# A two-layer vision tower in fp32 on one core: gelu rows weighted by GpSimd, layer 0's probabilities divided as rows, layer 1's projections merged and its loop written in another order

## The chip, the cores and the metric

The kernel runs on one core of a Trainium2 chip. The metric is the device time of one execution in microseconds (us), median of the runs. Engines are named as in the profile: PE is TensorE, DVE VectorE, ACT ScalarE, POOL GpSimd, SP the engine that issues the DMAs.

## What is computed

32 images give 38 tokens each (36 patches, two class tokens) of width 256. Two layers follow; each adds an attention part and a feed-forward part to the running activation `h`.

```python
h = tok(x) ; h = concat([cls_tok, h])                         # patches @ W.T + b, + positions
h = h + attn0(layernorm(h))        # rope(q), rope(k), causal softmax(q k^T * scale) @ v, then @ Wo.T ; 16 heads of 16
h = h + moe0(layernorm(h))         # 8 experts, no activation between w_in and w_out; softmax over the top 2
h = h + attn1(layernorm(h))        # full softmax; 8 value heads; 16x8 outputs mixed by a second softmax; Wf;
                                   # + relu MLP 256->512->256
def ffn1(x):                       # ternary weights: sign(W) where |W| > mean|W|/2, else 0
    g = gelu(x @ tern(W_fc).T)     # 1024 wide
    return (layernorm(g) * ln_w + ln_b) @ tern(W_proj).T
h = h + ffn1(layernorm(h))
```

## The kernel before

**Tiles.** Three images make a tile of R = 114 rows; there are T = 11 tiles, all resident in `h`. Every engine's program is written out by hand, with semaphores; steps of different tiles are interleaved so that PE always has something to do. A function such as `c2_qk(t)` exists in the program of each engine that takes part in step `c2` of tile `t`, and the order of the calls is the order of the instructions. A wait holds everything behind it on its engine.

**fp32 from two halves.** Most products run as three fp32r matmuls (`mm3`, L1895 to L1897): high half by high half, high by low, low by high. `turn_hi` (ACT, L518) writes the high half of a transposed tile to `xth`, `turn_lo` (DVE, L978) the low half to `xtl`. Transposes (L1909, L1978, L2263) and a few products are plain fp32; each of those stands as two matmuls in the trace.

**Stage A** (layer 0's attention, and the folding of each expert's two matrices into one). The loop over t = 2 to 7 is `a_step(t)`. On PE: `scores(t-1)`, the transpose of xn, half of `combine(t)` (L2010), q/k/v products, `turn_p` (L1978: the 16 heads' probabilities transposed in four groups through tb0 and tb1), the other half of `combine`, `a2_pv` (L1989: v times probabilities, output transposed, four column groups of the array at once; L1993: the sums of the probabilities, by a matrix of ones `hsum`), transposes of q and k, `a1_patch(t+1)`, `a2_wo(t-1)` (L1895 on tb). The softmax: DVE takes the maximum (L1041) and subtracts it (L1047), ACT takes exp three times, once per image of the tile, with a bias that makes the columns of the other images zero (L561), into `p_exp`. After `a2_pv` DVE takes the reciprocal of the sums (`a2_recip`, L1061) and multiplies (`a2_o`, L1066), ACT and DVE split the result (L575, L1070).

**Stage C** (experts `c1`, layer 1's attention `c2`, its MLP `c3`). The loop over i = 5 to 10 is `c_step(i)`, with tiles i to i-4 in it. `c1_gate` is a product 8 columns wide (a `product` on `wc`, six matmuls, then `gate(t,0)` copies it, L1234). `c2_qk` makes q and k (512 columns into tb1), `c2_v` v and two more columns sets (152 columns into tb0); ACT copies q and k to rows (L635), PE transposes them back. ACT scales the experts' outputs (L695), POOL adds them to `h` (L378).

**Stage D** (layer 1's feed-forward, straight-line code that begins inside the end of C). Per tile: `d1_x`, `d1_fc` (L2251, L2252), gelu on ACT (`d1_gelu`, L736) into the one buffer `gel`, `d2_turn` (L2263, eight transposes into the two banks of `score`), `d2_hi` (ACT, L748, eight instructions that also multiply by the layer norm's weight, one column of `lnwc` each), `d2_lo` (DVE, L1438, eight), `d2_proj` (L2273, L2274), `d2_centre` and `d2_out` (L1449, L1455). `d2_stats` (L1422) needs the gelu rows.

## Time and profile before

| | us |
|---|---|
| median of 3 runs (lowest, highest) | 544.42 (544.40, 547.71) |
| the profiled execution's own time | 544.11 |
| its span, first to last instruction | 542.3 |
| mean granted PE clock | 0.988 of full |
| busy: PE, DVE, ACT, POOL | 498.7, 380.1, 280.1, 194.8 |

The 1.8 us between span and time lie outside of the instructions. Busy times are of engines that work beside each other. A matmul's own duration overlaps with the next one's, so the pace of PE is read from the distance between starts.

### The profile page before, as it was taken

Reading aid. Unit: us, or ns where it says so; the run is one execution under the profiler, and the core shown is the slowest. Engines: PE = TensorE matmul, PEld = TensorE weight load, DVE = VectorE, ACT = ScalarE, POOL = GpSimd, SP = SyncE. Lnnn points to the kernel's source line nnn. Section 1 sums busy time; section 2 is a strip of 40 time slices with the busy share of each in tenths; the row PEclk is TensorE's granted clock in tenths of the full one; section 3 lists DMA queues with packets and bytes.
Section 4 is the critical chain, followed back from the end, with each engine's and each line's share of the span. In section 5 each row is a group of like instructions: output and inputs, shape, how many; then the busy total and the mean of one; then the engine's idle time right before and its main releaser. Section 6 shows DMA issues by size and latency. Waiting matters only on the chain. (4 is left out here: it accounts for less than half of the span.)

```text
span 542.3 us, 11847 instructions
## 1 busy us (share of the span) xinstructions
PE 498.7 (92%) x3814; PEld 418.8 (77%) x3814; DVE 380.1 (70%) x1009; ACT 280.1 (52%) x684; POOL 194.8 (36%) x257
## 2 busy tenths in 40 slices
PE   8989999999998888689999999999999998989994
PEld 8778877877786666468778888888888886877874
DVE  5554366466456767547898878778788787799884
ACT  4220321322223334547667776776776787665751
POOL 4232123132133311365464553543643601243311
PEclk9998999999999999999999999999999999999997
DMA  8934342432504100000000000000000000000000
GB/s 302 391 110 164 116 149 90 153 131 81 176 27 158 25 2 1 1 0 2 1 1 1 2 0 0 0 0 0 0 0 0 2 2 0 2 10 26 19 25 16
DMA packets 10992, 29.64 MB, mean 55 GB/s; under 512 B 2192, under 2 KB 3408, under 8 KB 10704
## 3 DMA queue, kind: packets, MB, share of 16 engines
q1 hardware_dynamic: 10960, 29.23, 16.0%
q8 instruction: 18, 0.29, 0.2%
q14 instruction: 14, 0.11, 0.1%
HBM read 27.98 MB, written 1.25 MB: 54 GB/s over the span
## 5 line engine op out<-in xcount | busy, mean ns | idle before, releaser
L378 POOL TENSOR_TENSOR h<-h,scaled 114x256 f32 (+1 forms) x88 | 68.5, 779 | 43.2 <-ACT scaled L695 36.5
L330 POOL TENSOR_TENSOR small<-small,half 114x1 f32<-114x1 f32 x44 | 28.6, 650 | 135.8 <-DVE small L966 135.8
L561 ACT ACTIVATE p_exp<-sc,cst 114x608 f32<-114x608 f32 x66 | 48.1, 794 | 26.8 <-DVE sc L1047 26.8
L2010 PE MATMUL bz<-ebuf 128*128 128x256 f32 x256 | 59.0, 383 | 0.0
L569 ACT ACTIVATE pt<-tb 114x456 f32<-114x456 f32 x66 | 34.4, 556 | 35.4 <-PE tb L1978 35.3
L2010 PEld LDWEIGHTS bz<-ebuf 128*128 128x128 f32 x256 | 47.9, 192 | 5.9
L1978 PE MATMUL tb<-cst,p_exp 114*114 114x114 f32 x352 | 44.1, 266 | 6.2 <-ACT pt L569 3.7
L2156 PE MATMUL score<-v,pt 114*114 114x137 f32 x352 | 48.5, 282 | 0.0
L695 ACT ACTIVATE scaled<-bank,gl 114x256 f32<-114x256 f32 x88 | 38.8, 471 | 18.1 <-PE bank L1897 10.3
L1978 PEld LDWEIGHTS tb<-cst,p_exp 114*114 114x114 f32 x352 | 35.2, 134 | 15.4 <-ACT pt L569 7.0
L2156 PEld LDWEIGHTS score<-v,pt 114*114 114x114 f32 x352 | 43.9, 178 | 1.8
L1960 PE MATMUL score<-k_exp,q_exp 64*114 64x152 f32 x528 | 41.7, 304 | 1.3 <-DVE k_exp L1261 1.3
L1960 PEld LDWEIGHTS score<-k_exp,q_exp 64*114 64x114 f32 x528 | 36.1, 178 | 6.4 <-issue 6.1
L1895 PE MATMUL bank<-we_h,xth 128*114 128x512 f32 x88 | 37.9, 430 | 1.4 <-ACT scaled L695 1.3
L518 ACT ACTIVATE xth<-bank 128x228 fp32r<-128x228 f32 x33 | 11.9, 362 | 45.9 <-PE bank L1909 42.1
L341 POOL TENSOR_TENSOR o<-o 114x512 f32<-114x512 f32 x11 | 14.0, 1272 | 59.7 <-DVE o L1027 59.7
L1896 PE MATMUL bank<-we_l,xth 128*114 128x512 f32 x88 | 35.0, 397 | 0.0
L1897 PE MATMUL bank<-we_h,xtl 128*114 128x512 f32 x88 | 35.0, 397 | 0.0
L662 ACT ACTIVATE o<-score 114x411 f32<-114x411 f32 (+1 forms) x66 | 31.5, 480 | 5.4 <-PE score L2156 4.5
L748 ACT ACTIVATE we_h<-score,lnwc 128x114 fp32r<-128x114 f32 x88 | 23.0, 373 | 15.1 <-PE score L2263 9.2
L2273 PE MATMUL tb<-wa,we_h 128*114 128x256 f32 x88 | 23.2, 299 | 6.2 <-DVE we_h L1438 6.2
L1041 DVE TENSOR_REDUCE smax<-score 114x16 f32<-114x608 f32 x22 | 17.3, 788 | 13.7 <-PE score L1960 13.7
(210 smaller groups left out, 1315.6 us busy)
## 6 DMA issues: line engine op xcount, KB each, us to landing
ebuf<-in_w_in SPq DMA_DIRECT2D x16, 512.0 KB, 4.3
ebuf<-in_w_out SPq DMA_DIRECT2D x16, 512.0 KB, 5.1
x_raw<-in_x_tiles SPq DMA_DIRECT2D x11, 342.0 KB, 3.1
out<-h SPq DMA_DIRECT2D x10, 114.0 KB
raw<-in_w_a SPq DMA_DIRECT2D x4, 256.0 KB, 4.2
ebuf<-in_fc SPq DMA_DIRECT2D x1, 1024.0 KB, 4.9
ebuf<-in_proj SPq DMA_DIRECT2D x1, 1024.0 KB, 7.0
raw<-in_w_a SPq DMA_DIRECT2D x2, 384.0 KB, 5.4
```

What stands on the lines that cost most here:

```text
L378: gp.tensor_tensor(h[0:R, t, :], h[0:R, t, :], scaled[0:R, e % 4, :], ALU.add).then_inc(moe_acc, 1)
L561: act.activation(p_exp[0:R, :, b * S:(b + 1) * S], sc[0:R], ACT.Exp, bias=cst[0:R, CB + b:CB + b + 1], scale=SCALE).then_inc(exps, 1)
L569: act.activation(pt[0:R, 4 * g:4 * g + 4, :], tb[g % 2][0:R, 0:4 * R].rearrange("p (h r) -> p h r", h=4), ACT.Copy).then_inc(pt_odd if g % ...
L662: act.activation(o1[0:R, h0:h0 + k, :], score[0:R, g % 2, 0:k * VE].rearrange("p (h d) -> p h d", h=k), ACT.Copy).then_inc(pv1_out, 1)
L695: act.activation(scaled[0:R, e % 4, :], bk[1 + e // 2 % 2][0:R, (e % 2) * D:(e % 2 + 1) * D], ACT.Copy, scale=gl[0:R, 7, e:e + 1]).then_in ...
L1895: pe.matmul(dst, lh, rh_, start=first, stop=False)
L1896: pe.matmul(dst, lh, rl_, start=False, stop=False)
L1897: return pe.matmul(dst, ll, rh_, start=False, stop=last)
L1960: last = pe.matmul(score[0:R, i, f * HQ * S:(f + 1) * HQ * S], q_exp[rows64, f].rearrange("p b x -> p (b x)")[:, b * R:(b + 1) * R], k_exp ...
L1978: last = pe.transpose(tb[g % 2][0:R, i * R:(i + 1) * R], p_exp[0:R, 4 * g + i, :], cst[0:R, CI:CI + R])
L2010: last = pe.matmul(bz[:, m * D:(m + 1) * D], ebuf[:, 0, c * D + m * P:c * D + (m + 1) * P], ebuf[:, 1, c * D:(c + 1) * D], start=(c == 0 a ...
L2156: last = pe.matmul(score[0:R, g % 2, i * VE:(i + 1) * VE], pt[0:R, place(h0 + i), :], v1[0:R, :], start=True, stop=True)
```

## The change

Five parts.

1. **Probabilities divided as rows (stage A).** ACT takes one exp over the dense 114x608 rows (`a2_exp`), DVE sums each head's row, inverts and multiplies (`a2_norm`, three instructions), ACT copies the rows three times into `p_exp` with a scale of 0 or 1 (`a2_wide`). The eight matmuls with `hsum` (16 in the trace), `a2_recip` and `a2_o` go; ACT and DVE split the output straight from PSUM (`a2_o`, `a2_lo`). In PE's loop a quarter of `combine` moves ahead of `a1_turn`.
2. **Merged products (stage C).** q, v and eight more columns are one product of 392 columns into tb1, k and 16 more one of 272 into tb0. The weights come in four DMAs for two, so `wc_in` counts to 112. `c2_qT` and `c2_kT` wait for both copies and for `c2_v` on DVE.
3. **Gate.** Four matmuls (16 columns, 8 columns, for each half) for six; DVE adds the two halves (a reduce for the copy).
4. **Gelu rows weighted (stage D).** POOL multiplies each half row of gelu by the weight row (`d2_weigh`, 114x512) into `gel_w`; `d2_turn` reads that. `d2_hi` and `d2_lo` become one instruction per half (128x456). `gel` has two buffers.
5. **Order.** `c_step` and all straight-line parts are written in another order on every engine; the two loops keep their bounds. `tern_sum(0)` is now ACT's first step after the stage A loop, `split_x(10)` stands ahead of `a1_rope(8)` on POOL.

```diff
@@ DVE @@
-            def a2_recip(t):
-                V.reciprocal(rinv0, score[:, 0, 2 * R:4 * R]).then_inc(rinv0_ready, 1)
-            def a2_o(t):
-                V.tensor_tensor(y2[:], two(score[:, 0, 0:2 * R]), two(rinv0), ALU.mult).then_inc(o_ready, 1)
+            def a2_norm(n, k):
+                if k == 0:
+                    dve.wait_ge(dense, n + 1)
+                    V.tensor_reduce(psum_rows[0:R, 0], sc[0:R], AX, ALU.add).then_inc(summed, 1)
+                elif k == 1:
...
+                    V.reciprocal(psum_rows[0:R, 1], psum_rows[0:R, 0]).then_inc(inverted, 1)
+                else:
...
+                    V.tensor_tensor(sc[0:R], sc[0:R], psum_rows[0:R, 1].unsqueeze(2).broadcast_to([R, H, S]),
+                                    ALU.mult).then_inc(scaled_rows, 1)
@@ ACT @@
+            def a2_exp(n):
+                act.wait_ge(shifted, 2 * n + 2)
+                act.activation(sc[0:R], sc[0:R], ACT.Exp, scale=SCALE).then_inc(dense, 1)
+            def a2_wide(n, batches=range(G)):
+                act.wait_ge(scaled_rows, n + 1)
...
+                    act.activation(p_exp[0:R, :, b * S:(b + 1) * S], sc[0:R], ACT.Copy,
+                                   scale=inside[0:R, b:b + 1]).then_inc(exps, 1)
@@ PE a_step @@
                 a1_v(t)
+                combine(t, (4, 5))
                 a1_turn(t - 1)
-                combine(t, (4, 5, 6, 7))
+                combine(t, (6, 7))
@@ PE c2 @@
             def c2_qk(t):
                 pe.wait_ge(t2["lo"], t + 1)
-                product(tb[1][0:R, :], xth[1], xtl[1], wc, C_QK, 2 * D, (0, 2 * D)).then_inc(qk1_mm, 1)
+                since(pe, pt_odd, 2 * (t + T))
+                product(tb[1][0:R, 0:WQ], xth[1], xtl[1], wc, C_QK, W4, (0, WQ)).then_inc(qk1_mm, 1)
             def c2_v(t):
-                pe.wait_ge(q_ready, 2 * (t + T) + 2)
-                product(tb[0][0:R, 2 * R:2 * R + W2], xth[1], xtl[1], wc, C_V, W2, (0, W2)).then_inc(v1_mm, 1)
+                pe.wait_ge(t2["lo"], t + 1)
+                product(tb[0][0:R, 0:D + H], xth[1], xtl[1], wc, C_QK, W4, (WQ, W4)).then_inc(v1_mm, 1)
@@ POOL @@
+            def d2_weigh(t, halves):
...
+                for q in halves:
+                    gp.wait_ge(gelu, 2 * t + q + 1)
+                    if q == 0:
+                        since(gp, gT_mm, 2 * t)
+                    cols = slice(q * 512, (q + 1) * 512)
+                    gp.tensor_tensor(gel_w[0:R, cols], gel[t % 2][0:R, cols], lnw_row[0:R, cols], ALU.mult).then_inc(weighted, 1)
@@ DVE d2_lo @@
-                    for c in range(4):
-                        k = 4 * q + c
-                        last = V.scalar_tensor_tensor(gtl[:, k, :], score[:, q, c * R:(c + 1) * R], lnwc[:, k:k + 1],
-                                                      gth[:, k, :].bitcast(F32), ALU.mult, ALU.subtract)
+                    V.tensor_tensor(gtl[:, 4 * q:4 * q + 4, :], score[:, q, 0:4 * R].rearrange("p (c r) -> p c r", c=4),
+                                    gth[:, 4 * q:4 * q + 4, :].bitcast(F32), ALU.subtract).then_inc(gT_lo, 1)
```

**PE in the loop of stage A**, from the last product for v (bank2) to the transposes of q and k; L1978 and L2031 are the transposes of the probabilities, L2010 and L2059 `combine`. In the kernel before:

```order
L1897 MATMUL bank2<-wa,xtl0 114x256
L1978 MATMUL tb0<-cst,p_exp 114x114 x4
L1978 MATMUL tb1<-cst,p_exp 114x114 x4
L2010 MATMUL bz<-ebuf 128x256 x8
L1989 MATMUL score<-pt,scaled 32x114 x16
L1993 MATMUL score<-pt,scaled 32x228 x8
L1909 MATMUL tb1<-cst,o1 128x114 x2
L1909 MATMUL bank1<-cst,o1 128x114 x2
```

The same place in the changed kernel:

```order
L1950 MATMUL bank2<-wa,xtl0 114x256
L2059 MATMUL bz<-ebuf 128x256 x4
L2031 MATMUL tb0<-cst,p_exp 114x114 x4
L2031 MATMUL tb1<-cst,p_exp 114x114 x4
L2059 MATMUL bz<-ebuf 128x256 x4
L2042 MATMUL score<-pt,scaled 32x114 x16
L1962 MATMUL tb1<-cst,o1 128x114 x2
L1962 MATMUL bank1<-cst,o1 128x114 x2
```

A quarter of `combine` (x4, eight matmuls in the trace) moved ahead of the transposes of the probabilities, a quarter is left behind them, and the matmuls with the ones (32x228) are gone.

**DVE in the same loop**, from the maximum of the scores to the low half of the attention's output (xtl1). In the kernel before:

```order
L1041 TENSOR_REDUCE smax<-score 114x16
L1047 TENSOR_TENSOR sc<-score,smax 114x304 x2
L978 TENSOR_TENSOR xtl0<-bank0,xth0 128x228
L1021 TENSOR_TENSOR o1<-bank1,cst 114x512
L1056 COPY pt<-tb1 114x456
L1078 TENSOR_TENSOR we_l<-bz,we_h 128x2x256
L1061 RECIPROCAL att<-score 128x228
L1066 TENSOR_TENSOR y2<-score,att 128x228
L1035 TENSOR_TENSOR k_exp<-bank1,cst 128x456
L1070 TENSOR_TENSOR xtl1<-y2,xth1 128x228
```

The same place in the changed kernel:

```order
L1092 TENSOR_REDUCE smax<-score 114x16
L1098 TENSOR_TENSOR sc<-score,smax 114x304 x2
L1029 TENSOR_TENSOR xtl0<-bank0,xth0 128x228
L1113 TENSOR_REDUCE psum_rows<-sc 114x16
L1116 RECIPROCAL psum_rows<-psum_rows 114x16
L1119 TENSOR_TENSOR sc<-sc,psum_rows 114x608
L1072 TENSOR_TENSOR o1<-bank1,cst 114x512
L1107 COPY pt<-tb1 114x456
L1132 TENSOR_TENSOR we_l<-bz,we_h 128x2x256
L1086 TENSOR_TENSOR k_exp<-bank1,cst 128x456
L1124 TENSOR_TENSOR xtl1<-score,xth1 128x228
```

The reciprocal and the product that stood between the expert's low half and the first half of k_exp are gone; three instructions on the 608 columns of `sc` stand ahead of rope (L1072), and the low half is now taken from `score`.

**ACT at the start of stage D**, from the softmax of tile 9 (p_exp) on; the load at L792 or L736 is for gelu, that at L595, L667 or L720 for exp. In the kernel before:

```order
L736 ACT_TABLE_LOAD
L736 ACTIVATE ebuf<-bank1 114x512
L736 ACTIVATE ebuf<-bank2 114x512
L667 ACT_TABLE_LOAD
L667 ACTIVATE mx<-mx 114x128
L736 ACT_TABLE_LOAD
L736 ACTIVATE ebuf<-bank1 114x512
L736 ACTIVATE ebuf<-bank2 114x512
L667 ACT_TABLE_LOAD
L667 ACTIVATE mx<-mx 114x128
L736 ACT_TABLE_LOAD
```

The same place in the changed kernel:

```order
L792 ACT_TABLE_LOAD
L792 ACTIVATE ebuf<-bank1 114x512
L595 ACT_TABLE_LOAD
L595 ACTIVATE p_exp<-sc,cst 114x16x38 x3
L792 ACT_TABLE_LOAD
L792 ACTIVATE ebuf<-bank2 114x512
L792 ACTIVATE ebuf<-bank1 114x512
L792 ACTIVATE ebuf<-bank2 114x512
L720 ACT_TABLE_LOAD
L792 ACT_TABLE_LOAD
L720 ACT_TABLE_LOAD
L792 ACT_TABLE_LOAD
```

Before there are five loads of a table behind the stage C loop, after there are seven.

## Rows read from the trace of the kernel before

**Rows 1.** Busy us in stretches: span, then PE, PEld, DVE, ACT, POOL; clock, DMA.

```profile
71.20:169.80 98.60, 93.29 (x821) 78.65 (x820) 54.20 (x106) 26.72 (x55) 26.74 (x30) 1.00 0.37 120
169.80:231.30 61.50, 48.68 (x515) 37.99 (x514) 41.70 (x100) 25.84 (x52) 18.70 (x23) 1.00 0.05 13
231.30:292.20 60.90, 56.35 (x375) 45.86 (x375) 46.90 (x124) 38.77 (x92) 34.67 (x37) 0.97 0.00 1
292.20:418.30 126.10, 126.10 (x891) 107.22 (x890) 101.32 (x295) 91.58 (x234) 58.88 (x84) 1.00 0.00 0
...
476.20:538.50 62.30, 54.06 (x356) 45.78 (x354) 52.77 (x180) 35.95 (x119) 19.96 (x32) 0.98 0.07 20
```

**Rows 2.** Who PE waited for, whole run: us in total, times, longest.

```profile
PE tb L2273 <- DVE we_h L1438: 6.2, 5, 2.9
...
PE bank L1909 <- DVE xn L971: 3.5, 8, 0.7
...
PE tb L1895 <- DVE xtl L1070: 2.0, 6, 0.3
```

**Rows 3.** Timeline of PE, one turn of the stage A loop: start, us, line.

```profile
101.19 3.63 PE L2010 MATMUL bz<-ebuf 128*128 128x256 f32 x16
...
105.56 0.95 PE L1993 MATMUL score<-pt,scaled 114*32 114x228 f32 x16
106.44 0.41 PE L1909 MATMUL tb<-cst,o 114*128 114x114 f32 x2
...
110.66 1.82 PE L1960 MATMUL score<-k_exp,q_exp 64*114 64x152 f32 x24
...
118.81 0.94 PE L1978 MATMUL tb<-cst,p_exp 114*114 114x114 f32 x8
...
120.92 3.63 PE L2010 MATMUL bz<-ebuf 128*128 128x256 f32 x16
```

**Rows 4.** Groups of instructions: xcount | busy us, mean ns | idle before.

```profile
L561 ACT ACTIVATE p_exp<-sc,cst 114x608 f32<-114x608 f32 x66 | 48.1, 794 | 26.8 <-DVE sc L1047 26.8
...
L569 ACT ACTIVATE pt<-tb 114x456 f32<-114x456 f32 x66 | 34.4, 556 | 35.4 <-PE tb L1978 35.3
...
L1438 DVE SCALAR_TENSOR_TENSOR we_h<-score,lnwc,we_h 128x114 fp32r<-128x114 f32 x88 | 22.7, 324 | 3.8 <-ACT we_h L748 3.8
...
L1061 DVE RECIPROCAL att<-score 128x228 f32<-128x228 f32 x11 | 17.4, 1583 | 4.0 <-PE score L1993 4.0
L1041 DVE TENSOR_REDUCE smax<-score 114x16 f32<-114x608 f32 x22 | 17.3, 788 | 13.7 <-PE score L1960 13.7
...
L341 POOL TENSOR_TENSOR o<-o 114x512 f32<-114x512 f32 x11 | 14.0, 1272 | 59.7 <-DVE o L1027 59.7
L1056 DVE COPY pt<-tb 114x456 f32<-114x456 f32 x22 | 13.9, 632 | 12.5 <-PE tb L1978 11.6
```

**Rows 5.** Timeline of PE in the stage C loop.

```profile
347.52 0.17 PE L1895 MATMUL bank<-wc,xth 128*114 128x8 f32 x1
...
348.04 0.31 PE L1895 MATMUL tb<-wc,xth 128*114 128x152 f32 x1
...
348.68 0.57 PE L1909 MATMUL bz<-cst,raw 114*128 114x114 f32 x4
...
359.52 0.39 PE L1896 MATMUL tb<-wc,xth 128*114 128x512 f32 x1
...
360.67 0.63 PE L2156 MATMUL score<-v,pt 114*114 114x137 f32 x4
```

**Rows 6.** Timeline of ACT in stage D.

```profile
474.55 1.28 ACT L736 ACT_TABLE_LOAD   x1 [2.42 <-issue]
...
528.02 1.26 ACT L736 ACTIVATE ebuf<-bank 114x512 f32<-114x512 f32 x2
531.98 2.08 ACT L748 ACTIVATE we_h<-score,lnwc 128x114 fp32r<-128x114 f32 x8 [2.70 <-PE score L2263]
```

**Rows 7.** Timeline of PE, the last tile's last product.

```profile
535.22 0.37 PE L2273 MATMUL tb<-wa,we_h 128*114 128x256 f32 x1 [2.88 <-DVE we_h L1438]
```

More of the change, by code:

```diff
@@ L584, in _ @@
             a1_x(0)
+            act.activation(inside[0:R], cst[0:R, CB:CB + G], ACT.Exp).then_inc(init, 1)
             a1_v(0)
@@ L733, in d1_gelu @@
                     if q == 0:
-                        since(act, gT_mm, 2 * t)
-                        since(act, g_stat, 4 * t - 2)
-                    act.activation(gel[0:R, q * 512:(q + 1) * 512], bk[1 + q][0:R, :], ACT.Gelu).then_inc(gelu, 1)
+                        since(act, weighted, 2 * t - 2)
+                        since(act, g_stat, 4 * t - 6)
+                    act.activation(gel[t % 2][0:R, q * 512:(q + 1) * 512], bk[1 + q][0:R, :], ACT.Gelu).then_inc(gelu, 1)
             def d2_hi(t, halves=(0, 1)):
@@ L1505, in _ @@
[L1505 removed]
+            gate(0, 0)
             plus_eps(n1, 1)
[L1507 to L1510 removed]
+            a1_k(10, (0,))
+            gate(0, 1)
+            a1_k(10, (1,))
+            a2_lo(9)
             c1_normed(1)
             c1_stats(2)
[L1513 to L1516 removed]
             gate(0, 2)
[L1518 removed]
+            gate(0, 3)
@@ L1707, in _ @@
             mix(8, 12)
-            d1_x(1)
+            normed1(10)
             d2_stats(0, (0,))
+            c2_x(10)
             d1_norm(2)
             d0_stats(3)
+            d1_x(1)
+            d2_stats(0, (1,))
+            c3_res(7)
+            c2_v(10, (0,))
+            aggr(nD, 3)
+            d2_aggr(0)
+            mix(9, 0)
+            mix(9, 1)
+            d2_eps(0)
+            plus_eps(nD, 3)
+            c2_v(10, (1,))
+            mix(9, 2)
+            c3_sum(8)
+            mix(9, 3)
@@ L1786, in _ @@
-            mix(10, 11)
-            aggr(nD, 6)
-            d2_out(0)
-            d1_x(4)
+            keep_bias()
+            d2_lo(0, (1,))
+            d2_stats(2, (1,))
+            aggr(nD, 6)
+            d2_aggr(2)
+            mix(10, 9)
+            d2_eps(2)
+            plus_eps(nD, 6)
+            keep_sums()
+            d2_centre(0)
+            d2_lo(1, (0, 1))
+            d1_x(4)
+            mix(10, 10)
+            d2_out(0)
+            mix(10, 11)
+            d1_norm(6)
@@ L1802, in _ @@
-            d2_out(1)
+            c3_stats(10)
+            d1_x(6)
+            aggr(n4, 10)
+            plus_eps(nD, 7)
+            d2_out(1)
+            plus_eps(n4, 10)
+            d1_norm(7)
+            d2_aggr(3)
+            c3_normed(10)
+            d2_eps(3)
+            d2_lo(3, (0, 1))
             d2_centre(2)
-            d2_lo(3, (0,))
-            aggr(nD, 7)
-            d2_lo(3, (1,))
+            d0_stats(8)
+            d2_stats(4, (0, 1))
+            aggr(nD, 8)
             d2_out(2)
-            d2_aggr(3)
@@ L2096, in c1_gate @@
                 pe.wait_ge(t1["lo"], t + 1)
-                product(bk[0][0:R, 256:256 + E], xth[0], xtl[0], wc, C_G, E, (0, E)).then_inc(gate_mm, 1)
+                for c in range(DC):
+                    pe.matmul(bk[0][0:R, 256:256 + 2 * E].rearrange("p (a e) -> p a e", a=2), xth[0][:, c, :],
+                              wc[:, :, C_G + c * E:C_G + (c + 1) * E], start=(c == 0), stop=False)
+                    last = pe.matmul(bk[0][0:R, 256:256 + E], xtl[0][:, c, :], wc[:, 0, C_G + c * E:C_G + (c + 1) * E],
+                                     start=False, stop=(c == DC - 1))
+                last.then_inc(gate_mm, 1)
             def c1_moe(t, pairs):
```

1158 lines of the change are left out of this document (579 added, 579 removed).

## The prediction

> **What bounds the kernel now.** I read the busy times by stretch first [rows 1], then what PE waited for [rows 2], then timelines where the change works, and last the groups for prices. The reader is to compare PE's busy time with each stretch's length. From 292.2 to 418.3 (the stage C loop, six turns of 21.0 us) PE is busy for all of 126.1 us: it sets the pace, and only taking work off PE, or a new wait, changes it. In the five turns of the stage A loop from 71.2 to 169.8 PE idles 98.6 - 93.3 = 5.3 us, 1.06 a turn. From 169.8 to 231.3, where stage A drains, it idles 12.8 us, from 231.3 to 292.2 4.6 us, and in the last stretch 8.2 us. So PE bounds the loops; between them and at the end chains over DVE and ACT do. In the waits, stage D shows as PE waiting 6.2 us for the low halves of gelu, 2.9 of them once, and stage A as PE waiting for xn (0.44 on average) and for the low half of the attention's output (0.33) [rows 2].
>
> **The sum** is made against the profiled execution's 544.1 us; the median is 0.3 above that.
>
> **Stage A's loop.** One turn takes 120.92 - 101.19 = 19.73 us [rows 3]. Removed on PE: the matmuls with the ones, from 105.56 to 106.44, 0.88 us. Removed on DVE: the reciprocal of 1.58 us [rows 4] and a product of about 0.4; both stand between `a2_pv` and `a2_wo`, and ahead of `a1_k` and the moments of the next tile. With nearly 2 us gone from that path, the wait of `a2_wo` (0.33) and that for xn (0.44) end [rows 2]. Saved: 0.88 + 0.33 + 0.44 = 1.65 us a turn, 9.9 in six turns; tile 0, outside of the loop, gives 0.9.
>
> The price is on the other side of the tile: the softmax. From the end of the scores (110.66 + 1.82 = 112.48) to the transposes of the probabilities (118.81) PE has 6.3 us of other work [rows 3]; the quarter of `combine` put ahead of them adds 3.63 / 2 = 1.8, so the cover is 8.1 us. Behind it must fit: maximum 0.79 and subtraction, about as long, exp 0.79 once, sum 0.79 (as the maximum of the same 608 columns), inversion 0.2, product 0.8, three copies of 0.79 [rows 4]: 6.6 us, and with six handoffs of 0.1 (my estimate) 7.2. It fits with 0.9 to spare, so I cost it at nothing here. The unseen ones are bounded by rows: the copy between 0.56 (456 columns) and 0.79 (the exp, 608 columns), the product between 0.63 (456 columns) and 1.6 (the reciprocal's price), each taken by the row nearest in columns. At the upper end the chain is 8.0 and still fits; what isn't covered comes back six times.
>
> **Where stage A drains** (tiles 7 to 10) that cover is thin, and the chain is the time: per tile it gains 0.79 + 0.79 + 0.2 + 0.8 = 2.6 us and handoffs, and loses 0.88 + 1.58 + 0.4 = 2.9. I take the two as equal. `tern_sum(0)`, now ACT's first step, and POOL's `split_x(10)` ahead of `a1_rope(8)` each hold a chain by some 2 us there, which the other of the two partly covers. Against that, two of the experts' products of tile 0 now stand in a wait for the softmax, and the gate of tile 0 too. I take 1.3 us saved; the ends are 4 lost and 5 saved, of the 12.8 us idle.
>
> **Stage C, all eleven tiles.** Six matmuls of 8 columns take 0.52 us, six of 152 columns 0.64, so neither costs in proportion to its columns: a step lasts 0.09 to 0.11 at least. One of 512 columns takes (360.67 - 359.52) / 5 = 0.23 [rows 5]. Now: gate 4 steps for 6, 0.17 less. Merged products: 6 x 0.23 + 0.64 = 2.02 before; after, 392 and 272 columns in proportion to 512, 6 x (0.176 + 0.122) = 1.79, 0.23 less. Together 0.40 a tile, 4.4 in eleven. Since PE never idles in this loop, all of it shows if no wait comes. The transposes of q and k now wait for two copies by ACT and both sums by DVE, but an expert's product of 1.4 us (6 x 0.23) was put between. In the straight-line turns (4.6 us idle [rows 1]) the same cover stands where PE waited; I take 1.2 saved, between 1 lost and 3 saved.
>
> **Stage D.** `d2_hi` is eight instructions in 2.08 us [rows 6], `d2_lo` eight in 8 x 0.26 = 2.06 (22.7 / 88 [rows 4]). After: two each; ACT's at 0.56 (the same 456 columns), DVE's at 0.63, its copy of 456 columns; the dearest row for it is four of 0.324, 1.3. DVE, 52.8 of 62.3 us busy, gets 0.8 us a tile free, ACT 1.0. From the start of `d2_hi` to the product that needs the last `d2_lo` it now takes 535.22 - 531.98 = 3.24 us [rows 6, 7]; after, 0.56 + 0.56 + 0.63 + handoffs = 1.95. That is 1.3 less for each tile. PE's waits there are 3.3 us in four and 2.9 in the last [rows 2]: the four go, the last falls by 1.3. That gives 4.6, and 0.9 of the idle left comes with it: 5.5 us.
>
> Added is POOL's work: 2 x 1.27 us a tile (114x512, the same shape as `a1_rope`'s [rows 4]), 28 us in all, on an engine with 20.0 of 62.3 us used in the last stretch. It lies between gelu and the transposes. For the last tile gelu ends at 529.3 [rows 6], so the second product would end near 531.9, with its transposes at 532, where they end now: hidden. With a second gelu buffer, gelu of the next tile doesn't wait.
>
> The Trainium skill speaks against this part: its GPSIMD Engine Reference, section 4.1, sends elementwise products to VectorE, since GpSimd is about twice as slow with two inputs. The trace has 1.27 us on POOL for 512 columns, and DVE's product would not be half the problem, as DVE is the fuller engine; by that rule the first rival would decide.
>
> Two more loads of an activation table stand in the new order. One lasts 1.28 us [rows 6]; ACT idles enough there, so nothing to 2.6 us, taken as nothing. The Trainium skill (ScalarE: Activation LUTs, What ACT_TABLE_LOAD costs) adds a drain of 1.38 us to each load; 2.42 us of idle stand ahead of the one in the rows, which agrees in kind. By it ACT would lose 5.3 us, not 2.6.
>
> **Sum:** 0.9 + 9.9 + 1.3 + 4.4 + 1.2 + 5.5 = 23.2; 544.1 - 23.2 = 520.9, with the 0.3 of the median 521.2; I say 521.
>
> **Rivals.**
> 1. POOL sets the pace of stage D. For: 2.54 us a tile on top of two powers and an addition, in an engine that works in order; if DVE's use of memory slows it to 2 us a product, it needs over 5.5 us a tile, as now. Against: it idles two thirds of the stretch. Then stage D gives nothing, 521 + 5.5 = 526.5.
> 2. The softmax isn't covered. For: six handoffs, and DVE does other steps between. Against: 0.9 us to spare. With 1 us of wait in ten tiles 531.
> 3. In stage C the transposes wait for the copies, 0.6 us a tile, 528. For: three engines in a row within 1.4 us. Against: ACT was built in right ahead.
> 4. More goes than I count: the drain of stage A gives its 5, stage D its 8.2. 515. For: both idle sums exist. Against: chains are left in both.
> 5. Slower: in the stage C loop the new order makes a ring, where DVE's `c2_v(1)` stands behind `mix(0)`, that behind ACT's copy of the last attention output, and PE's transposes behind all. From 23.2 / 11 = 2.1 us of wait a tile on it eats the gain. At 3 us it costs 33, 554. For: none of these waits existed, and PE had no idle in 126 us, so each adds in full. Against: by the rows each link is under 0.6 us.
>
> **Chances.** Forecast 0.61, rival 1 0.14, rival 2 0.07, rival 3 0.07, rival 4 0.05, rival 5 0.06, a third of it beyond 550. A measurement of this kernel can tell about 1%, 5.4 us, from no change: faster than 539, slower than 550. Faster 0.94, within 1% 0.04, slower 0.02. The range of 8 in 10 takes in rivals 1 to 4 and the unknown prices: 512 to 532.
>
> **What would show it.** Right: no 32x228 matmuls; turns of 18.1 us in stage A's loop and of 20.6 in stage C's, with PE still busy throughout; DVE's low halves of gelu as 22 instructions of 0.6 us; under 3 us idle in PE's last stretch before the final tile. Wrong: PE waiting for p_exp inside stage A's loop (rival 2), for the rows or for v ahead of the transposes (3, 5), or for POOL's products in stage D (1).

## The result, and the profile after

The changed kernel takes 553.19 us (median of 13 runs, 548.02 to 555.67), the kernel before 544.27 in as many; the ratio is 1.0142, with a 95% interval of 1.0113 to 1.0170. It is slower by 1.4%, where 521 us had been forecast. The profiled execution has a span of 553.1 us at a mean granted PE clock of 0.958; before it was 542.3 us at 0.988. Executions of one program differ with the granted clock (five of these 13 took 548.0 to 549.9 us at 0.967 to 0.975, the other eight, the profiled one among them, 552.1 to 555.7 at 0.958 to 0.963), and the ratios leave out those over 1.5% above the fastest of their kernel (two of e1's ten, one of e8's).

The stretches of the changed kernel first (columns as in [rows 1]): the same five turns of the stage A loop, the way from the scores of tile 7 to the small product for the ternary sums (tb<-th,ones), the stage C loop, then up to the scores of tile 10, and the rest.

```profile
72.60:164.50 91.90, 88.14 (x742) 75.90 (x740) 54.01 (x111) 29.56 (x60) 26.73 (x30) 1.00 0.38 124
164.53:237.57 73.04, 54.56 (x446) 44.26 (x445) 38.59 (x95) 27.99 (x55) 16.93 (x21) 0.81 0.06 18
298.60:426.20 127.60, 126.43 (x878) 108.50 (x877) 102.09 (x296) 95.02 (x240) 71.44 (x84) 1.00 0.00 0
426.20:460.80 34.60, 31.09 (x207) 27.02 (x205) 25.03 (x78) 26.70 (x61) 15.51 (x19) 0.95 0.00 1
460.80:553.10 92.30, 79.38 (x529) 67.65 (x528) 72.16 (x169) 44.77 (x95) 52.04 (x59) 0.97 0.05 15
```

- The loop of stage A does what was forecast, nearly: 91.9 us for five turns where [rows 1] has 98.6.
- From the scores of tile 7 to the ternary sums it takes 73.0 us; before, the same way was 169.85 to 231.14, 61.3 us, at a clock of 1.00. Now PE idles 73.0 - 54.6 = 18.5 us there and gets a clock of 0.81. That is the largest change of the whole trace, and in the wrong direction.
- The stage C loop takes 127.6 us for six turns, 126.0 before; PE is busy for 126.4 of them, and yet the turns are slower.
- From the scores of tile 10 to the end it takes 92.3 us for 95.6 (446.7 to 542.3 before).

Summed by these marks, after minus before, in us: the start (to the scores of tile 1) +2.8, the loop of stage A -8.1, between the loops +11.7, unrolled stage C -0.2, its loop +1.6, from there to the scores of tile 10 +6.2, the rest -3.3; in all +10.7, for 10.8 between the spans.

The last two of these sums don't hold the same work. The new order has eight matmuls of 512 columns of `d1_fc` ahead of the scores of tile 10 that stood behind them before (L2251 and L2252 80 times behind the mark, L2310 and L2311 72 times); at 0.23 us each that is 1.9 us moved from one stretch to the other. Without them it is +4.3 up to the scores of tile 10 and -1.4 for the rest. Taken together, the two take 126.9 us for 124.0.

Who PE waited for (as [rows 2]):

```profile
PE bank L1948 <- DVE xtl L1029: 6.2, 3, 3.2
PE tb L2031 <- ACT p_exp L614: 6.1, 3, 2.8
...
PE tb L2031 <- issue: 4.0, 3, 3.3
...
PE score L2322 <- DVE we_h L1496: 2.0, 3, 1.1
```

Three more lines of before belong beside these:

```profile
PE score L1955 <- DVE y L1066: 2.6, 2, 1.8
PE tb L1978 <- ACT p_exp L561: 2.4, 2, 1.6
...
PE score L2263 <- DVE we_h L1438: 1.8, 2, 1.1
```

Three waits for `p_exp` (L614) take 6.1 us, where two took 2.4 (L561), and one for the softmax of tile 9 (put down as "issue") takes 3.3. The two waits for the attention's output behind the reciprocal and the product (y, L1066), 2.6 us, are gone. The wait for the low halves of gelu was 6.2 us at the product [rows 2] and 1.8 at the transposes (L2263), and is 1.7 (L2332) and 2.0 (L2322) now; but PE waits 2.7 us for gelu itself (ebuf, L792), which no line of before has.

### The profile page after: what moved, and what is told of

It is laid out like the page before. It is cut to its first block, busy times and chain, and to the rows that moved or that the text cites. A ratio compares the mean times of both kernels' runs of the same rounds, so it can differ in the third digit from the quotient of the medians.

```text
span 553.1 us, 11435 instructions
## 1 busy us (share of the span) xinstructions
PE 499.7 (90%) x3616; PEld 425.2 (77%) x3616; DVE 378.0 (68%) x954; ACT 282.2 (51%) x643; POOL 234.9 (42%) x277
## 4 chain that ended last, share of the span: by engine, by line
PE 42%; ACT 5%; DVE 4%; issue 4%; POOL 0%; DVEq 0%; ACTq 0%; POOLq 0%
PE score L2215 7%; PE bz L2245 3%; PE tb L2031 3%; PE score L2013 3%; PE bank L1948 2%; PE bank L1950 2%; PE bank L1949 2%; PE tb L2332 2%; PE bank L2310 2%; PE tb L2333 2%; PE bz L1962 2%; PE bank L2311 2%; PE bz L2227 2%; PE score L2322 1%; PE bz L1948 1%
## 5 line engine op out<-in xcount | busy, mean ns | idle before, releaser
L2059 PE MATMUL bz<-ebuf 128*128 128x256 f32 x256 | 60.1, 384 | 0.0
L2031 PE MATMUL tb<-cst,p_exp 114*114 114x114 f32 x352 | 47.4, 281 | 13.4 <-ACT p_exp L614 6.1
L2031 PEld LDWEIGHTS tb<-cst,p_exp 114*114 114x114 f32 x352 | 37.9, 142 | 22.7 <-ACT p_exp L614 6.7
L2059 PEld LDWEIGHTS bz<-ebuf 128*128 128x128 f32 x256 | 47.6, 193 | 5.7
L2013 PE MATMUL score<-k_exp,q_exp 64*114 64x152 f32 x528 | 43.0, 310 | 0.1
L2013 PEld LDWEIGHTS score<-k_exp,q_exp 64*114 64x114 f32 x528 | 37.6, 185 | 5.5 <-issue 4.5
L614 ACT ACTIVATE p_exp<-sc,inside 114x608 f32<-114x608 f32 x33 | 24.1, 794 | 21.5 <-DVE sc L1119 21.5
L715 ACT ACTIVATE o<-score 114x411 f32<-114x411 f32 (+1 forms) x66 | 31.3, 479 | 7.3 <-PE score L2215 5.8
L430 POOL TENSOR_TENSOR ebuf<-ebuf 114x512 f32<-114x512 f32 x22 | 28.3, 1296 | 12.2 <-PE score L2322 9.3
L345 POOL TENSOR_TENSOR small<-small,half 114x2 f32<-114x2 f32 x11 | 21.9, 1991 | 21.6 <-DVE small L1249 21.6
L1107 DVE COPY pt<-tb 114x456 f32<-114x456 f32 x22 | 13.9, 632 | 25.0 <-PE tb L2031 25.0
```

The costliest lines, as they stand in the source:

```text
L715: act.activation(o1[0:R, h0:h0 + k, :], score[0:R, g % 2, 0:k * VE].rearrange("p (h d) -> p h d", h=k), ACT.Copy).then_inc(pv1_out, 1)
L2013: last = pe.matmul(score[0:R, i, f * HQ * S:(f + 1) * HQ * S], q_exp[rows64, f].rearrange("p b x -> p (b x)")[:, b * R:(b + 1) * R], k_exp ...
L2031: last = pe.transpose(tb[g % 2][0:R, i * R:(i + 1) * R], p_exp[0:R, 4 * g + i, :], cst[0:R, CI:CI + R])
L2059: last = pe.matmul(bz[:, m * D:(m + 1) * D], ebuf[:, 0, c * D + m * P:c * D + (m + 1) * P], ebuf[:, 1, c * D:(c + 1) * D], start=(c == 0 a ...
```

## Where the time went

**The loop of stage A** by the row of PE that comes once a turn, `combine` behind the transposes of the probabilities:

```profile
103.03 1.26 PE L2059 MATMUL bz<-ebuf 128*128 128x256 f32 x5
...
121.41 1.90 PE L2059 MATMUL bz<-ebuf 128*128 128x256 f32 x8
```

The turn is 121.41 - 103.03 = 18.38 us, where [rows 3] has 19.73: 1.35 us saved, for 1.65 forecast. PE has no wait for `p_exp` in it.

**The exit of that loop.** ACT and PE, tile 8:

```profile
167.32 1.91 ACT L667 ACTIVATE raw<-ebuf 128x2048 f32<-128x2048 f32 x1 [5.25 <-POOL wc L357]
169.13 0.19 ACT L667 ACTIVATION_READ_ACCUMULATOR raw<-ebuf 128x1 f32 x1
169.23 0.34 ACT L552 ACTIVATE xth<-bank 128x228 fp32r<-128x228 f32 x1
...
172.13 2.19 ACT L614 ACTIVATE p_exp<-sc,inside 114x608 f32<-114x608 f32 x3 [1.97 <-DVE sc L1119]
```

```profile
170.14 0.53 PE L1948 MATMUL bank<-wa,xs 128*114 128x256 f32 x1 [3.19 <-DVE xtl L1029]
170.47 0.42 PE L1949 MATMUL bank<-wa,xs 128*114 128x256 f32 x1
```

`tern_sum(0)` (1.91 and 0.19 us) stands ahead of the high half of tile 8 (169.23), and PE waits 3.19 us. The matmul of 256 columns behind that wait starts every 0.21 us for 0.12 before: PE came out of the wait at 1.2 GHz, half its clock, and stayed there until 175.8, 5.7 us.

**The softmax of tile 10**, on DVE and on ACT:

```profile
217.53 0.79 DVE L1092 TENSOR_REDUCE smax<-score 114x16 f32<-114x608 f32 x1 [2.54 <-PE score L2013]
...
219.99 0.79 DVE L1113 TENSOR_REDUCE psum_rows<-sc 114x16 f32<-114x608 f32 x1 [0.78 <-ACT sc L608]
...
221.10 0.79 DVE L1119 TENSOR_TENSOR sc<-sc,psum_rows 114x608 f32<-114x608 f32 x1
```

```profile
219.25 0.71 ACT L608 ACTIVATE sc<-sc 114x608 f32<-114x608 f32 x1 [5.21 <-DVE sc L1098]
221.93 2.19 ACT L614 ACTIVATE p_exp<-sc,inside 114x608 f32<-114x608 f32 x3 [1.97 <-DVE sc L1119]
```

From the start of the maximum to the end of the third copy: 221.93 + 2.19 - 217.53 = 6.6 us. Before, the same chain ran from 214.89 to 218.80, 3.9 us. The 2.7 us more are what the prediction had worked out (2.6; of its handoffs of 0.1 us each the rows have 0.03 to 0.05). PE can't cover all of them: it waits 2.82 us for 1.56 before, comes out at half the clock, and runs the 16 transposes in 3.51 us, where [rows 3] has eight in 0.94:

```profile
224.17 3.51 PE L2031 MATMUL tb<-cst,p_exp 114*114 114x114 f32 x16 [2.82 <-ACT p_exp L614]
```

**Stage D's first gelu** on ACT:

```profile
439.83 1.28 ACT L792 ACT_TABLE_LOAD   x1 [1.73 <-PE bank L2311]
441.12 0.60 ACT L792 ACTIVATE ebuf<-bank 114x512 f32<-114x512 f32 x1
441.74 1.28 ACT L595 ACT_TABLE_LOAD   x1
443.03 2.19 ACT L595 ACTIVATE p_exp<-sc,cst 114x608 f32<-114x608 f32 x3
```

The load for gelu, half a gelu, the load back for exp, and only then the exps of tile 9, which PE waits 3.26 us for; it then runs at half its clock from 445.3 to 448.8. The prediction had seen the two loads and taken them as nothing.

**Groups of the changed kernel** (columns as [rows 4]):

```profile
L430 POOL TENSOR_TENSOR ebuf<-ebuf 114x512 f32<-114x512 f32 x22 | 28.3, 1296 | 12.2 <-PE score L2322 9.3 <-ACT ebuf L792 2.9
...
L345 POOL TENSOR_TENSOR small<-small,half 114x2 f32<-114x2 f32 x11 | 21.9, 1991 | 21.6 <-DVE small L1249 21.6
...
L1496 DVE TENSOR_TENSOR we_h<-score,we_h 128x456 fp32r<-128x456 f32 x22 | 13.2, 625 | 3.5 <-ACT we_h L801 3.1
...
L801 ACT ACTIVATE we_h<-score 128x456 fp32r<-128x456 f32 x22 | 11.3, 551 | 13.4 <-PE tb L2333 9.9 <-PE score L2322 3.6
L1119 DVE TENSOR_TENSOR sc<-sc,psum_rows 114x608 f32<-114x608 f32 x11 | 9.9, 903 | 0.4
```

The prices of the sum were right: DVE's low half of gelu 0.63 us (L1496; [rows 4] has eight of 0.32 a tile for it), ACT's high half 0.55, POOL's product 1.30 (1.27 for the same shape in [rows 4]), the division of 608 columns 0.90 (I had 0.8), the dense exp 0.71 (0.79). No price of an instruction failed; what failed is what lies beside them.

## The experiments

All times are medians of interleaved runs beside the kernel before (544.0 to 544.1 us in each group). "Between the loops" is always the way from the scores of tile 7 to the ternary sums, from each profiled execution.

| kernel | us | ratio to before (95%) | between the loops, us | clock there |
|---|---|---|---|---|
| before | 544.3 | 1 | 61.3 | 1.00 |
| changed | 553.2 | 1.0142 (1.0113 to 1.0170) | 73.0 | 0.81 |
| e1 two ACT steps back | 546.8 | 1.0039 (1.0009 to 1.0069) | 72.6 | 0.81 |
| e8 e1, and PE's a1_qk(8) first | 546.7 | 1.0046 (1.0018 to 1.0074) | 69.6 | 0.85 |
| e5 changed, dummies in the gaps | 541.7 | 0.9961 (0.9936 to 0.9985) | 64.2 | 1.00 |
| e12 e5, and gelu back | 538.5 | 0.9908 (0.9873 to 0.9943) | 64.2 | 1.00 |
| e2 before, rows in every tile | 554.8 | 1.0165 (1.0118 to 1.0213) | 79.7 | 0.78 |
| e14 e2, dummies in the gaps | 547.1 | 1.0076 (1.0047 to 1.0105) | 69.2 | 1.00 |
| e15 before, the same dummies | 551.6 | 1.0153 (1.0121 to 1.0185) | 69.4 | 1.00 |
| e6 before, rows in the loop only | 536.7 | 0.9868 (0.9839 to 0.9898) | 61.3 | 1.00 |
| e10 new order, rows in the loop only | 554.3 | 1.0183 (1.0159 to 1.0208) | 76.1 | 0.89 |
| e3 before, gelu weighted on POOL | 542.2 | 0.9958 (0.9938 to 0.9978) | | |
| e4 before, gate of four | 542.6 | 0.9976 (0.9951 to 1.0000) | | |
| e7 changed, without the weighting | 562.7 | 1.0332 (1.0299 to 1.0366) | | |
| e11 two waits of the C loop | 552.8 | 1.0170 (1.0140 to 1.0200) | | |
| e13 changed, gate of six | 552.0 | 1.0163 (1.0128 to 1.0199) | | |
| e9 e6 + e4 + e3 | 533.6 | 0.9821 (0.9787 to 0.9854) | 60.9 | 1.00 |

**e1: two of ACT's steps put back.**

```diff
-            tern_sum(0)
             a1_x(8)
             a2_exp(7)
             a2_wide(7, (0, 1, 2))
             a1_pt(7, (0, 2))
+            tern_sum(0)
...
             c1_scale(10, (7,))
-            d1_gelu(0, (0,))
             softmax_exp(9 + T, (0, 1, 2))
...
             c2_hi(10)
+            d1_gelu(0, (0,))
```

> The changed kernel with two of ACT's steps back where they stood: tern_sum(0) behind a1_pt(7), and the first half of gelu of tile 0 behind c2_hi(10), past the softmax of tile 9. Theory O (the new order on ACT costs the time): both idle times of PE behind the two loops, 3.2 and 3.3 us, go, and with them the two stretches at half clock that begin there (3.4 us each, 1.7 us of work each): 8 to 9 us less than the changed kernel, 544 to 546 us. Theory R (the longer softmax chain between the loops costs it): the waits behind it stay, so 2 to 4 us less, 549 to 551.

546.8 us, between what the two theories had. In the trace the gelu step gave 2.7 us (from the scores of tile 9 to those of tile 10), the other next to nothing: 72.6 us between the loops for 73.0. Theory O had both stretches at half clock last 3.4 us; the rows above have 3.5 us at 445.3, but 5.7 at 170.1.

```profile
PE bank L1948 <- POOL xs L335: 2.7, 1, 2.7
```

PE now waits 2.7 us for POOL's split of x at the place where it waited 3.2 us for ACT. The medians are 6.4 us apart, the two profiled spans only 2.9 (553.1 and 550.2). Both of these have a clock of 0.91 in their first 60 us, so the steps are judged by the stretches of the trace: together they are worth some 3 us.

**e8: and the step of PE behind it.**

```diff
             a1_x(8)
-            a1_patch(9)
             a1_qk(8)
+            a1_patch(9)
```

> Run e1 with one more step back in PE's program: a1_qk(8) ahead of a1_patch(9), as before, since in e1 PE waited 2.7 us for POOL's split of x for tile 9 there. Theory O: that wait goes and a stretch at half clock with it, 2 to 4 us less than e1's 546.8, 543 to 545. Theory R: the wait is only moved to the transposes of tile 7's probabilities, 546 to 547.

546.7 us, no different from e1, as theory R had it; but in the profiled execution the stretch gets 3.0 us shorter (69.6 for 72.6, at a clock of 0.85 for 0.81). The three steps together give back 3.4 us of the 11.7 between the loops, so they are not the main part of what costs there.

**e2: the row-wise division alone, in the old order.** Part 1 of the diff in the kernel before; `a2_norm(n, 0..2)` stands behind each `softmax_sub(n)`, the calls of `a2_recip` and `a2_o` are gone.

```diff
             softmax_max(8)
             softmax_sub(8, (0, 1))
+            a2_norm(8, 0)
+            a2_norm(8, 1)
+            a2_norm(8, 2)
             a1_rope(9, (0,))
```

> The kernel before, in its own order, with part 1 alone (probabilities divided as rows, and a quarter of combine ahead of the transposes). Theory R: the loop of stage A turns in 18.4 us for 19.7, 8 us less in six turns, but each of the four tiles 7 to 10 gets 2.5 us more between its scores and its transposes, the first two tiles 3 us together, and stretches at half clock follow: 13 us or more given back, 546 to 552 us. Theory O: this part keeps its gain, 532 to 537 us.

554.8 us, more than either theory had, and no better than the whole change. The loop still gains 8.2 us, and 18.4 us are lost between the loops:

```profile
164.50:244.23 79.73, 58.12 (x450) 45.70 (x449) 40.05 (x104) 28.21 (x56) 18.17 (x23) 0.78 0.05 17
```

```profile
PE tb L2005 <- ACT p_exp L578: 8.6, 4, 4.2
```

Four waits for `p_exp`, one a tile, the longest 4.2 us, at a clock of 0.78. So in the old order this part alone makes the kernel slower, and between the loops by more than the whole change does.

**e6: rows in the loop, columns outside of it.** The kernel before, where `a_step` (tiles 1 to 6) divides as rows and tiles 0 and 7 to 10 keep three exps, the matmuls with the ones, reciprocal and product:

```diff
+        COL = {0: 0, 7: 1, 8: 2, 9: 3, 10: 4}
+        by_col = lambda t: isinstance(t, int) and t in COL
...
-                for e in range(2):
+                for e in range(2 if by_col(t) else 0):
...
             def a_step(t):
                 a1_x(t)
-                softmax_exp(t - 1)
+                a2_exp(t - 1)
+                a2_wide(t - 1)
```

> The kernel before, in its own order, with the probabilities divided as rows only in the loop (tiles 1 to 6); tiles 0 and 7 to 10 keep the matmuls with the ones, the reciprocal and the product. Theory R (the longer softmax costs only where nothing covers it): 1.35 us less in each of six turns and nothing given back, 8 us less than before, 535 to 537 us. If the part's cost sits in the loop or its exit: 542 us or more.

536.7 us. The loop's gain stays whole, and between the loops the stretch is the old one:

```profile
161.30:222.62 61.32, 48.44 (x513) 37.80 (x513) 41.49 (x100) 25.83 (x52) 18.55 (x23) 1.00 0.07 22
```

61.3 us at the full clock, as before. In the old order the same instructions gain 8 us where PE has work to cover them and lose 18 where it hasn't enough.

**e5, e14, e15: what the clock costs.** Dummy matmuls (`warm(n)`, ones by ones into `bz`, which nobody reads then) ahead of PE's waits:

```diff
             a1_x(8)
+            pe.wait_ge(we_lo, E)
+            warm(13)
             a1_patch(9)
...
+            warm(11)
             a1_turn(10, (0, 1, 2, 3))
```

> The changed kernel with dummy matmuls (ones by ones, 128x128, into bz, which nothing reads there) put ahead of eight waits of PE between the two loops: 13, 9, 8, 4, 4, 11, 4 and 9 of them, each row about as long as the wait that it fills. No engine does less work and no chain gets shorter. Theory K (the idle times cost twice, since PE runs at half clock for 3.4 us behind them): the mean clock rises from 0.958 to 0.97 or more, and the time falls by 4 to 9 us, 544 to 549. If the chains alone cost the time: no change, or slower by the dummies that overrun their wait, 553 to 556.

541.7 us: 11.5 us less than the changed kernel, with 62 matmuls more (124 in the trace) and none of its chains shorter. This is below the kernel before. The stretch between the loops, in e5:

```profile
159.81:223.98 64.17, 56.48 (x551) 47.90 (x551) 38.65 (x95) 27.89 (x55) 16.57 (x20) 1.00 0.07 21
```

64.2 us at 1.00 for 73.0 at 0.81. So of the 11.7 us lost there, at least 8.8 come from the clock, and at most 2.9 from the chains (the dummies may have a share in these, see e15). From the ternary sums on e5 takes 315.3 us, the changed kernel 315.5. The profiled spans are 13.8 us apart (553.1 and 539.3); the other 4.7 lie ahead of the scores of tile 7, where the two programs are the same: a clock of 0.91 over the first 60 us in the changed kernel's execution, 1.00 in e5's, 0.97 before. So not all of the 11.5 us between the medians need be the dummies' work; what they gave is read from the stretch, 8.8 us, which is in the range forecast (4 to 9).

> Run e2 (rows in every tile, old order) with dummy matmuls in eight of PE's gaps between the loops (6, 4, 6, 9, 6, 10, 3 and 17, sized by e2's waits). Theory K: e2 lost 20 us between the loops, of which 2.7 us a tile are chain and the rest clock; filled, 8 to 11 us come back, 544 to 547 us. If the chain alone costs: 553 to 555.

547.1 us, 7.7 of e2's 554.8 back (8 to 11 were forecast), and the full clock between the loops here too.

> The kernel before with the same 61 dummies at the same places (some 13 us of PE work). Its gaps there are 12.8 us in all and no stretch at half clock follows them, so theory K gives no gain: the same time, or slower by the dummies that overrun, 544 to 550 us. A gain of over 2 us would say that dummies help for another reason.

These are the 61 dummies of e14. 551.6 us, 7.5 slower, and more than the 550 of the forecast:

```profile
169.70:239.08 69.38, 61.29 (x635) 51.67 (x635) 41.72 (x100) 25.70 (x52) 18.54 (x23) 1.00 0.04 11
```

The dummies cost 8.1 us between the loops, where the clock was at 1.00 anyway, so they help only by the clock, and e14 with its 69.2 us understates what the clock cost there.

**e10: the new order with the old softmax.** As e6, but in the changed kernel (`a2_recip` and `a2_o` stand ahead of each `a2_lo`).

> The changed kernel, in its new order, but tiles 0 and 7 to 10 divided as before (three exps, matmuls with the ones, reciprocal and product ahead of a2_lo). Theory R: nearly all of the 12.7 us lost between the loops comes back, 540 to 543 us. Theory O (the new order costs there too, whatever the softmax): half or less comes back, 546 to 550.

554.3 us, beyond what either theory had: nothing comes back, and the stretch between the loops gets longer, 76.1 us for 73.0. PE's waits name a reason:

```profile
PE score L2023 <- DVE y L1136: 6.2, 3, 2.9
```

In the new order `scores(t + 1)` follows close behind `a2_pv(t)`; the old softmax has a reciprocal and a product of 2 us on DVE between the two. In the old order PE waited 2.6 us for them in two of these tiles (L1066 above), here 6.2 in three. I had expected the order to be neutral here, and it isn't: with the old softmax it takes 76.1 us for 61.3, with the row-wise division 73.0 for 79.7. So in the new order no run shows that the division costs time between the loops; what is shown there is that the order fits it better, and that neither pair is as good as the old order with the old softmax.

**e3 and e7: the weighting on POOL, in either order.** e3 is part 4 of the diff in the kernel before, with `d2_weigh` put where the trace has the gelu rows ready. e7 takes `d2_weigh` out of the changed kernel; the splits get back their eight instructions with `lnwc`, and `gel` has three buffers.

```diff
-                    pe.wait_ge(weighted, 2 * t + q + 1)
+                    pe.wait_ge(gelu, 2 * t + q + 1)
...
-                    act.activation(gth[:, 4 * q:4 * q + 4, :], score[:, q, 0:4 * R].rearrange("p (c r) -> p c r", c=4),
-                                   ACT.Copy).then_inc(gT_hi, 1)
+                    for c in range(4):
+                        k = 4 * q + c
+                        last = act.activation(gth[:, k, :], score[:, q, c * R:(c + 1) * R], ACT.Copy, scale=lnwc[:, k:k + 1])
+                    last.then_inc(gT_hi, 1)
```

> The kernel before, in its own order, with part 4 alone (gelu rows weighted on POOL, one instruction per half for the two splits, two gelu buffers; POOL's steps put by the times of the trace). If stage D gains what the prediction said: 5.5 us less, 539 us; if POOL's two products set the pace there, or the load of the weight row waits: 544 us or more.

> The changed kernel without POOL's products: the layer norm's weights go back into the two splits (eight instructions of each), the transposes read the gelu rows themselves, which now have three buffers. If POOL's products pace stage D in the new order: faster than the changed kernel by 2 us or more, 551 or less. If they are hidden and the short splits gain what the prediction said: slower by 3 to 5 us, 556 to 558.

e3: 542.2 us, 1.8 less, between the two forecasts; e7: 562.7, 9.5 more than the changed kernel, where 3 to 5 had been forecast. In e3 PE waits for POOL instead of DVE:

```profile
PE score L2282 <- POOL ebuf L424: 5.4, 6, 2.7
```

In e7 it waits for DVE and ACT all over stage D:

```profile
PE score L2301 <- DVE we_h L1474: 6.7, 6, 1.8
...
PE bank L2289 <- ACT ebuf L765: 5.0, 3, 2.9
```

The part is worth 1.8 us in an order made for the long splits and 9.5 in one made for the short ones. Neither is its price alone. (From the scores of tile 10 to the end e7's trace takes 103.2 us, the changed kernel's 92.3.)

**e4 and e13: the gate.** e4 is part 3 in the kernel before, e13 the changed kernel with the old gate.

> The kernel before with part 3 alone (gate of four matmuls for six, a reduce for the copy). In the loop of stage C PE has no idle time, so 0.17 to 0.2 us in each of eleven tiles, 2 us less, 542.5 us; if the matmuls were hidden in waits anyway, no difference.

> The changed kernel with the gate of before (six matmuls of 8 columns for four, a copy for the reduce), 0.2 us more work for PE in each turn of the stage C loop. If PE's work paces the loop: turns of 21.4 us for 21.2, 2 us more than the changed kernel in all, 555. If a ring over ACT and DVE paces it (theory W after e11): the turn stays at 21.2 and the time at 553.

e4: 542.6 us, 1.5 less, which is the forecast (its interval reaches to no change). But the loop doesn't show it: its turn is (407.72 - 302.83) / 5 = 20.98 us, before (407.31 - 302.31) / 5 = 21.00. The gate gets 0.20 us shorter, and some 2 us later that is lost again: the transposes of the probabilities start 0.39 us behind the step ahead of them in e4, 0.24 before (350.25 to 350.49). In e4:

```profile
350.57 0.40 PE L1897 MATMUL bank<-we_h,xtl 128*114 128x512 f32 x1
350.96 0.99 PE L1978 MATMUL tb<-cst,p_exp 114*114 114x114 f32 x8
```

So the number came out, but not by the mechanism forecast, and where the 1.5 us come from isn't shown. e13: 552.0, in four executions from 547.7 to 554.0, which can't be told from the changed kernel's; its turn of the stage C loop is (408.30 - 301.89) / 5 = 21.28 us, where the changed kernel has 21.23. Two more matmuls of some 0.1 us each move the turn by 0.05: PE's work alone paces neither the old loop nor the new.

**e11: two waits in the loop of stage C.**

```diff
@@ DVE c_step @@
+                plus_eps(n4, i - 4)
                 c2_v(i - 2, (0,))
                 mix(i - 3, 0)
-                plus_eps(n4, i - 4)
@@ PE c_step @@
-                c3_wf(i - 4)
                 c2_pv(i - 3, (3,))
+                c3_wf(i - 4)
```

> The changed kernel with two steps of the stage C loop moved: DVE's plus_eps(n4) ahead of c2_v (behind it, it stands for 1.7 us, and PE's c3_x starts 0.35 us late), and PE's c3_wf behind one more group of c2_pv (it starts 0.2 us late). Theory W (the merged products and the gate save their 0.4 us a turn, and new short waits take 0.6 back): the turn falls from 21.2 to 20.7 us, 3 us less than the changed kernel in six turns, 549 to 551 us. If the merged products themselves save nothing: the turn stays above 21.0, 552 to 553.

552.8 us, and a turn of (415.02 - 308.66) / 5 = 21.27 us: no gain. Both waits shrank (c3_wf 0.90 us to 0.68, the transposes 0.3 less), and `c2_pv` grew from 3.62 us to 4.14:

```profile
363.31 0.91 PE L2215 MATMUL score<-v,pt 114*114 114x137 f32 x6
364.41 0.95 PE L2215 MATMUL score<-v,pt 114*114 114x137 f32 x6 [0.19 <-ACT o L715]
```

The group at 364.41 waits for ACT's copy (L715) of the group two before it, which used to happen behind `c3_wf`. The merged products themselves save PE what was forecast, in the changed kernel:

```profile
345.27 0.43 PE L1948 MATMUL tb<-wc,xth 128*114 128x392 f32 x1
...
346.43 1.10 PE L2215 MATMUL score<-v,pt 114*114 114x137 f32 x8
347.27 0.38 PE L1948 MATMUL tb<-wc,xth 128*114 128x272 f32 x1
...
348.11 0.39 PE L1948 MATMUL bank<-we_h,xth 128*114 128x512 f32 x1
```

392 columns: 346.43 - 345.27 = 1.16 us; 272 columns: 0.84; together 2.00, where the old pair took 1.58 + 0.64 = 2.22 in the loop. The products save PE 0.22 us a turn and the gate 0.20, and the turn is 0.23 us longer than before, so some 0.65 us of new short waits are in it. In e11 the ring PE - ACT - PE through the two halves of `score` takes what the two moves gave; which chain sets the turn of the changed kernel isn't shown.

**e12: e5 with the gelu step back.**

> Run e5 (dummies in PE's gaps) with the first half of gelu of tile 0 back behind c2_hi(10). PE's wait of 3.3 us for the softmax of tile 9, which the two table loads and the gelu stand ahead of, and the stretch at half clock behind it (1.7 us of work) go: 3 to 5 us less than e5's 541.7, 537 to 539 us. If the gelu is then late for its own users: 541 to 542.

538.5 us, as expected: 3.2 us less than e5 (3.4 from the scores of tile 9 to those of tile 10), and no wait takes the place of the one removed.

**e9: what works, together.** The kernel before, its order, rows in the loop only, the gate of four, the weighting on POOL.

> The kernel before, in its own order, with three parts: rows only in the loop (as e6), the gate of four matmuls (as e4), the gelu rows weighted on POOL (as e3). They work in three stages, so their gains should add: 7.3, 1.5 and 1.8 us less, 533 to 535 us. If one only shifts the others' waits: 536 or more.

533.6 us, 1.8% faster than before and 3.5% faster than the change; the three gains add up in the medians (7.3 + 1.5 + 1.8 = 10.6, measured 10.5).

From the scores of tile 10 to the end (436.90 to 529.70) it takes 92.8 us, 95.6 before:

```profile
436.90:529.70 92.80, 80.33 (x539) 68.45 (x538) 75.72 (x181) 46.52 (x96) 51.82 (x61) 1.00 0.05 15
```

PE idles 92.8 - 80.3 = 12.5 us there, at a clock of 1.00; before, it was 95.6 - 81.9 = 13.7 us at 0.97.

## Why the prediction was wrong

- **"With nearly 2 us gone from that path ... 9.9 in six turns".** Right in mechanism, a little large: 8.1 (1.35 a turn). PE still waits 0.5 us for xn in each turn, and 0.25 for a copy.
- **"The softmax ... It fits with 0.9 to spare, so I cost it at nothing here".** Right for the loop. "What isn't covered comes back six times" was the wrong place to look.
- **"Where stage A drains ... I take the two as equal ... I take 1.3 us saved".** This is the step that failed: measured +11.7 for -1.3. It set the lengths of the two chains against each other, 2.6 us for 2.9, and not what PE waits for at the end of each. Before, PE waited 2.4 us for `p_exp` and 2.6 for the reciprocal and the product. With the longer softmax in the old order (e2) the waits for `p_exp` are 8.6 us and the stretch loses 18.4; with it in the loop alone (e6) nothing is lost. In the changed kernel they are 6.1 us, none is left for the product, and `tern_sum(0)` holds PE for another 3.2, which the step had called partly covered. By e5 all that lengthens the chains there costs at most 2.9 us; the greater part is the next point. And by e10 the division isn't the cause by itself in the new order, which takes still longer with the old softmax.
- **No term for the clock.** The sum counted idle time once. At least 8.8 of the 11.7 us are PE at half its clock at and behind the waits (e5), the largest single loss. [rows 1] had 0.97 in one stretch and 0.98 in the last, each with idle times in it, and the sum gave neither a price.
- **"Two more loads ... taken as nothing".** Measured: +6.2 us up to the scores of tile 10, of which 1.9 are work moved there and one step of ACT gives 2.7 back (e1) or 3.4 (e12 against e5); its place, ahead of a softmax that PE waits for, decided, and not ACT's idle share. The bound of 2.6 us was for the loads alone, without the gelu between and without the clock.
- **"4.4 in eleven. Since PE never idles in this loop, all of it shows if no wait comes".** Merged products 0.22 a turn and the gate's 0.20 are gone from PE (rows above), and short waits take more: 21.23 us a turn for 21.00. The premise fails in the old order too, where the gate's 0.20 gives 0.02 (e4): a PE that is busy all the time can have a chain right behind it, and the row of busy times doesn't show that. The new waits are those of the third rival in size (0.6 a turn; it had 528), and in the place of the fifth, at a fifth of its price.
- **Stage D, 5.5.** Mis-sized: 3.3 us less from the scores of tile 10 on, of which 1.9 are work moved ahead of the mark, so 1.4 for 5.5. DVE's steps and PE's waits for them became what was said (8.0 us of waits for the low halves are 3.7), but PE's idle time in the stretch only fell from 13.7 to 12.9 us, since it now waits 2.7 us for gelu on ACT. The first rival (POOL paces it) holds in part in the old order (e3, 1.8 us gained), not in the new (e7). The Trainium skill's rule that elementwise products belong on VectorE, which the prediction had weighed, wasn't tried: no run puts these products on VectorE. e7 folds them back into the splits on ACT and DVE, and that costs 9.5 us.
- **The second rival** (the softmax isn't covered) named a right mechanism, with 1 us in ten tiles; the waits for `p_exp` grew by 3.7 us, between the loops alone, and the clock came on top. The fifth, the only slower one, was at the wrong place.

## What to carry to other kernels

Before a chain is made longer in exchange for a shorter one, look at every stretch in which it occurs, and ask in each whether PE waits at that end: in the old order the same edit gained 8 us in the loop and lost 18 where the loop drains. Price an idle time of PE by the row behind it, not by its length alone: where the matmuls behind it come at twice their usual distance, the wait costs more than its length, and dummies in the gap show it in one run. Before a stretch's time is compared, count the matmuls in it: a new order moves work across the mark. A busy PE doesn't prove that PE's work sets the pace (e4). And a hand-written order belongs to the parts it was written for: try an edit in both orders before you judge either.
